# Fourteen weight remainders by an accumulating DMA, and the last router scores one slot later

## The reference

```
x = x + block1(layernorm(x))     # 4 experts, picked by token id; weights ctx (256 x 256) for gate, up and down
x = x + block2(layernorm(x))     # 8 experts of width 176, top 2 of the router's scores, softmax weights
block: y = (silu(h @ W1.T) * (h @ W2.T)) @ W3.T
```

## Time and profile before

| what | us |
|---|---|
| median of 3 runs | 164.11 (164.03 to 164.11) |
| the profiled execution | 164.04 |
| its span, first to last instruction | 162.2 |
| PE busy with matmuls | 154.5 |
| VectorE busy | 111.7 |
| ScalarE busy | 67.8 |
| POOL busy | 57.2 |

### The profile page before, as it was taken

How to read it: one execution, slowest core, us unless ns; L and a number is a source line. 1 busy time by engine, 2 the same in 40 slices (tenths; PEclk the granted TensorE clock), 3 DMA queues, 4 the chain that set the end, 5 groups by cost and what they waited for, 6 DMA issues and landing times.

```text
span 162.2 us, 2463 instructions
## 1 busy us (share of the span) xinstructions
PE 154.5 (95%) x904; PEld 131.0 (81%) x904; DVE 111.7 (69%) x224; ACT 67.8 (42%) x121; POOL 57.2 (35%) x50
## 2 busy tenths in 40 slices
PE   7999899899999999999999799999999999999991
PEld 2477698789897788888889488888888888888890
DVE  0878999785986756799999947917444744444453
ACT  3385775754618622474335812324222222222210
POOL 0679956469767480555467310000000000000000
PEclk9999999999999999999999999999999999999999
DMA  3976353032030003033000000000000300000003
GB/s 107 349 246 191 82 203 107 0 97 76 29 97 0 2 0 101 0 97 97 0 4 0 0 0 2 4 0 0 0 0 4 129 0 0 0 2 4 0 0 129
DMA packets 4620, 8.76 MB, mean 54 GB/s; under 512 B 768, under 2 KB 1408, under 8 KB 4608
## 3 DMA queue, kind: packets, MB, share of 16 engines
q1 hardware_dynamic: 4176, 8.34, 16.3%
q10 hardware_dynamic: 432, 0.27, 0.5%
HBM read 7.55 MB, written 1.05 MB: 53 GB/s over the span
## 4 chain that ended last, share of the span: by engine, by line
PE 65%; DVE 21%; issue 4%; ACT 4%; POOL 3%; DVEq 0%; ACTq 0%; POOLq 0%
PE z L685 36%; PE y L710 22%; DVE act L587 5%; PE z L720 4%; DVE act_lo L552 4%; DVE norm L485 2%; DVE w_lo L558 2%; POOL gated L337 2%; DVE stats L468 2%; DVE hT_lo L492 1%; ACT act_hi L388 1%; ACT silu L416 1%; POOL rstd L299 1%; PE y L627 1%; DVE x_sb L498 1%
## 5 line engine op out<-in xcount | busy, mean ns | idle before, releaser
L685 PE MATMUL z<-hT_hi,w_hi 128*128 128x512 f32 x120 | 47.4, 395 | 1.1 <-ACT hT_hi L362 0.9
L685 PE MATMUL z<-hT_hi,w_lo 128*128 128x512 f32 x120 | 47.1, 393 | 0.0
L710 PE MATMUL y<-w_hi,act_lo 128*128 128x256 f32 x152 | 43.5, 286 | 1.0 <-DVE act_lo L552 0.9
L552 DVE TENSOR_TENSOR act_lo<-act,act_hi 128x512 fp32r<-128x512 f32 x38 | 33.6, 884 | 14.8 <-ACT act_hi L388 14.5
L710 PE MATMUL y<-w_hi,act_hi 128*128 128x256 f32 x152 | 43.0, 283 | 0.0
L710 PE MATMUL y<-w_lo,act_hi 128*128 128x256 f32 x152 | 42.9, 283 | 0.0
L416 ACT ACTIVATE silu<-z 128x512 f32<-128x512 f32 x38 | 22.6, 595 | 41.1 <-PE z L685 41.1
L685 PE MATMUL z<-hT_lo,w_hi 128*128 128x512 f32 x120 | 37.3, 392 | 0.0
L289 POOL TENSOR_TENSOR w_lo<-raw,w_hi 128x768 fp32r<-128x768 f32 (+1 forms) x15 | 27.5, 1845 | 20.3 <-ACT w_hi L353 18.9
L388 ACT CAST act_hi<-act 128x512 fp32r<-128x512 f32 x38 | 23.4, 617 | 19.7 <-DVE act L587 19.4
L710 PEld LDWEIGHTS y<-w_hi,act_lo 128*128 128x128 f32 x152 | 29.0, 191 | 3.2 <-DVE act_lo L552 1.5
(11 more groups left out here) (52 smaller groups left out, 80.8 us busy)
## 6 DMA issues: line engine op xcount, KB each, us to landing
raw<-weights_dram SPq DMA_DIRECT2D x11, 384.0 KB, 3.1
raw<-weights_dram SPq DMA_DIRECT2D x8, 256.0 KB, 4.5
x_sb<-x_dram SPq DMA_DIRECT2D x4, 256.0 KB, 4.4
out_dram<-x_sb SPq DMA_DIRECT2D x2, 256.0 KB, 2.5
out_dram<-x_sb SPq DMA_DIRECT2D x2, 128.0 KB, 2.0
out_dram<-x_sb ACTq DMA_DIRECT2D x2, 128.0 KB, 2.1
consts_sb<-consts_dram SPq DMA_DIRECT2D x1, 68.0 KB, 3.7
ids_sb<-token_ids_dram ACTq DMA_DIRECT2D x1, 4.0 KB, 3.9
```

The source lines that it names most:

```text
L552: nc.vector.tensor_tensor(act_lo[:, i, :], act[:, i, :], act_hi[:, i, :].bitcast(F32), ALU.subtract)\
L685: return nc.tensor.matmul(bank[:], w[b][:, c, cols], tokens[:, h, k, :], **flags)
L710: last = nc.tensor.matmul(o, a[:, q % BUFFERS, rows], w[b][:, c, wd], start=(first and j == 0), stop=(c == CHUNKS[b] - 1 and j == 2), skip ...
```

## The change

After it VectorE subtracts (0,0) alone, POOL (0,1) to (0,4), and the other 14, (0,5) to (0,7) and all 11 of block 2, are made in two moves. ScalarE, right after it has rounded the piece, writes the rounded piece negated into `w_lo` (a Copy with scale -1 into a float32r tile). Then POOL, where it would have subtracted, issues a DMA that adds the piece's weights from DRAM to that tile. `up` waits for the DMA's own semaphore. SP's reload of a raw buffer now waits for the negated pass instead of the remainder. (1,3) is no longer put off by a step on POOL. Apart from this, the last scores (half 1 of block 2) go from slot 0 to slot 1 of step 23, that is behind down(20).

```diff
-    "scores": (None, (7, 0), (7, 0)),
+    "scores": (None, (7, 0), (7, 1)),
...
-VECTOR_LO = ((0, 0), (0, 5), (0, 6), (0, 7))
-
-
-LATE_LO = (1, 3)
+VECTOR_LO = ((0, 0),)
+POOL_LO = ((0, 1), (0, 2), (0, 3), (0, 4))
+
+
+def by_dma(b, c):
+
+
+    return (b, c) not in VECTOR_LO + POOL_LO
+
...
+        w_lo_in = [[sem(f"w_lo_in{b}_{c}") if by_dma(b, c) else None for c in range(CHUNKS[b])] for b in range(2)]
+        w_negated = sem("w_negated")
...
         def wait_lo(engine, b, c):
 
-            vector = [p for p in VECTOR_LO if p <= (b, c)]
             if (b, c) in VECTOR_LO:
-                engine.wait_ge(w_lo_vector, len(vector))
+                engine.wait_ge(w_lo_vector, VECTOR_LO.index((b, c)) + 1)
+            elif (b, c) in POOL_LO:
+                engine.wait_ge(w_lo_pool, POOL_LO.index((b, c)) + 1)
             else:
-                engine.wait_ge(w_lo_pool, piece_no(b, c) - len(vector))
+                engine.wait_ge(w_lo_in[b][c], 16)
+
+        def negated_no(b, c):
+
+            return piece_no(b, c) - len(VECTOR_LO) - len(POOL_LO)
...
+                    last = (0, n) if n < CHUNKS[0] else (1, n - CHUNKS[0])
+                    if by_dma(*last):
+
+                        sp.wait_ge(w_negated, negated_no(*last))
+                    else:
+                        wait_lo(sp, *last)
...
+            def add_weights(b, c):
+
+                pool.wait_ge(w_negated, negated_no(b, c))
+                nc.gpsimd.dma_start(w_lo[b][:, c, :], (weights1, weights2)[b][:, c, :], accum_op=ALU.add)\
+                    .then_inc(w_lo_in[b][c], 16)
...
-                if LATE_LO in SPLIT_AT.get(q - 1, ()):
-                    weight_lo(*LATE_LO)
                 for piece in SPLIT_AT.get(q, ()):
-                    if piece not in VECTOR_LO and piece != LATE_LO:
+                    if by_dma(*piece):
+                        add_weights(*piece)
+                    elif piece in POOL_LO:
                         weight_lo(*piece)
...
                 nc.scalar.copy(w_hi[b][:, c, :], raw_piece(b, c)).then_inc(w_hi_done, 1)
+                if by_dma(b, c):
+                    nc.scalar.activation(w_lo[b][:, c, :], raw_piece(b, c), ACT.Copy, scale=-1.0).then_inc(w_negated, 1)
```

More of the change, by code:

```diff
@@ L252, in load_piece @@
                     n = piece_no(b, c) - RING - 1
-                    wait_lo(sp, *((0, n) if n < CHUNKS[0] else (1, n - CHUNKS[0])))
+                    last = (0, n) if n < CHUNKS[0] else (1, n - CHUNKS[0])
[3 more added lines that the diff above has]
+                        wait_lo(sp, *last)
                 sp.dma_start(raw_piece(b, c), (weights1, weights2)[b][:, c, :]).then_inc(w_in[b][c], 16)
@@ L324, in _ @@
             for c in range(FIRST_PIECES):
-                if (0, c) not in VECTOR_LO:
+                if (0, c) in POOL_LO:
                     weight_lo(0, c)
```

## The result

| | before | changed |
|---|---|---|
| median of 20 runs, us | 164.25 (164.03 to 165.06) | 166.18 (164.65 to 167.09) |
| ratio, 95% interval | | 1.0104 (1.0080 to 1.0129) |
| profiled execution / its span | 164.04 / 162.2 | 165.29 / 163.5 |
| PE, DVE, ACT, POOL busy | 154.5, 111.7, 67.8, 57.2 | 154.6, 103.0, 77.1, 46.2 |

The forecast was 163.4, range 162.3 to 165.2, with 0.23 on slower. The changed kernel's runs fall into two groups: 9 of 164.65 to 165.87 us at a granted clock of 0.996 or more, and 11 of 166.13 to 167.09 at 0.985 to 0.99. The two groups' medians are 165.53 and 166.87. The profile is of the first group. It can explain the 1.25 us by which it is longer than the profiled execution before, out of 1.93 between the medians; most of the rest comes from the second group.

A forecast was written before the change was run, and what follows sets the result against it. TensorE, busy 154.5 of 162.2 us, was taken as the bound. Delay 0.57 and scores -1.27 gave -0.7 us: 163.3 from the profiled 164.04, with the median 0.07 higher 163.4, range 162.3 to 165.2.

The forecast's parts named there:

- The unit costs: TensorE: six products of a block 1 up step 1.39 us, twelve of block 2 2.75, a down step 1.43.
- the list of holes: TensorE waits before down(1) 0.86, up(8) 0.84, down(11) 0.63 and the last scores 1.27: about 3.6 us to win.
- The last scores: Last scores moved behind down(20): either part alone cures the hole before them, together they cure it once, -1.27 us.
- ScalarE: 14 added negated passes, 0.55 us for 128x512 and 0.74 for 128x768, 9.8 us in sum; (1,0)'s on the path to up(8).
- the walk: Steps 1 to 3 followed engine by engine with an issue of 0.9 us: up(8) at 33.05, 1.2 us later.
- The issue, d: Time POOL takes to issue one DMA: taken as 0.9 us, between 0.46 and 1.85.
- rival B: POOL's issue is dear, 1.85 us, in front of gated in steps 1 to 3: up(8) +2.8, total 165.0; chance 0.15.
- So act_lo(1) runs 18.2 to 18.9: VectorE, without w_lo(0,5), does act_lo(1) unhindered; down(1) starts at 19.36 and its 0.86 hole closes.
- I take 4.5 and a bit and cost it at nothing: Landing of (0,5) by DMA, from POOL's taking up the issue at 17.9: costs nothing up to 5.9 us.
- rival C: The accumulating DMA lands late, 9.0 us after 17.9: up(8) 4.3 late, total 166.5; chance 0.09.
- From there the old spacing holds: After gated(5), 0.47 late, spacing unchanged but for the new 0.74 pass: up(8) at 33.05, 1.2 us later.
- The hole closes: +1.2 - 0.63: Before down(11): act_lo(11) ready near 51.8, TensorE asks at 52.3, so the delay from there on is +0.57.

The follow-up runs named there:

- e1: Kernel before with only the last scores moved behind down(20): 162.94 us, ratio 0.9913.
- e10: Changed kernel with (0,5), (0,6), (0,7) back on VectorE and (1,0) on POOL, so DMA for (1,1) to (1,10) only: 162.54 us, ratio 0.9889.
- e11: Kernel of e10 with (0,7) by DMA too, SP's loads of (1,1) and (1,2) held until it has landed: 161.98 us, ratio 0.9840.
- e2: Changed kernel with the last scores back in slot 0, ahead of down(20): 166.75 us, in two groups of runs.
- e9: Kernel of e7 with a POOL product of 128x512 in each probe step, in even steps behind an accumulating issue: act 2.50 us in step 28.
- e13: Kernel of e9 with POOL started from up(q) and two or three small products ahead of the issue: act_lo 2.62 us in one even step.
- e7: Kernel of e1 with eight 256 KB DMAs added on POOL in steps 28 to 35, accumulating and plain in turn: 162.85 us.
- e5: Changed kernel with SP's loads of (1,1) and (1,2) held until (0,6) landed: 8 of 13 runs 163.72 to 164.08 us, five 168.2 to 168.9.
- e12: Changed kernel where POOL issues (0,6), ahead of gated(3), only when act_lo(1) is done: 165.41 us.
- e6: Changed kernel with POOL's 14 DMAs as plain copies, the addition left out: 162.79 us.
- e3: Changed kernel with (0,5), (0,6), (0,7) back on VectorE, only block 2's pieces by DMA: 163.35 us, ratio 0.9929.
- e8: Changed kernel where POOL issues (0,5) only once act_lo(1) is done: 168.92 us.
- e4: Changed kernel with block 2's eleven remainders back on POOL, only (0,5), (0,6), (0,7) by DMA: 166.81 us.

## Why the prediction was wrong, step by step

**The unit costs and the list of holes: right.** e1 won what the last of the four holes holds, and e10 closed the third as well. The first two still stand in e10 (0.58 and 0.59 idle). The whole 3.6 us was reached by no run; e11 came to 2.5.

**The last scores: right.** -1.27 forecast; down(11) to up(24) took 43.08 - 41.85 = 1.23 less. e1 and e2 show that each part alone does it.

**ScalarE: right.** (0,5)'s pass, silu(2) and act_hi(1) came within 0.1 us of the walk; act of the second block fell to 0.68 (mean of 22).

**The issue, d: near, and on the high side.** 0.9 forecast; POOL's next instruction starts 0.83 after the first issue and 0.62 after the others. A dear issue (rival B) wasn't the cause.

**"So act_lo(1) runs 18.2 to 18.9": the first step that failed.** It took 2.67 us, and down(1) came at 20.88 instead of 19.36. I had used the rule that a two-operand VectorE instruction stands while POOL runs a product, and looked only at whether a product *was running* at 18.2. With the issue in front, the product that stood next in POOL's queue already kept it out (e9 and e13; the issue by itself doesn't, e7). The Trainium skill ("SBUF — State Buffer", section "Who interferes with whom") says that a VectorE instruction with two SBUF inputs contends with a GpSimd instruction that reads SBUF, and that the order of issue decides who blocks. The rows agree: in the kernel before, act_lo starts 0.11 us first, keeps its 0.68 and the product stands; in e9's odd steps the product is first, keeps its 1.29, and act_lo stands. That a queued product counts from the issue in front of it on is what e9 and e13 add.

In the profiled execution this hold cost the total nothing that shows: PE stood 1.71 us before up(5) as well, for the DMA, and would only have stood there longer. It costs where it happens twice. In 11 of 20 runs act_lo(1) presumably lost to gated(3) too: this is seen in e2's and e5's profiles, and gone in e12. PE then idles 3.4 us, its granted clock falls to the lower level of 1.2 GHz (e2: 0.64, 0.50, 0.50 and 0.65 in the four us from 24), and the run is 1.3 us longer (group medians 165.53 and 166.87). The prediction had no such case.

**"I take 4.5 and a bit and cost it at nothing": the second, and the one that decides.** (0,5) landed 6.4 us after POOL took it up (17.87 to 24.23), past the limit of 5.9 that the step itself set. (0,6), for which the prediction worked out no limit, took 7.6 (19.96 to 27.60). So PE idled 1.71 and 0.29 us, and up(8) started at 34.27, 2.42 late instead of 1.2. Of the 1.22 between, 0.47 is up(5) past 23.8, 0.44 the wait for (0,6), and 0.31 slower first products. That was rival C, at 0.09, in a milder form than priced. The mistake was to read the earlier trace rows's DMA slices of before as the company of the new transfers, and the median of SP's landings as theirs. Even these were read too low: the 5 in that row means 50 to 60%, and from 20 to 24 us the share was 0.61, where the prediction held against rival C that "no slice of the DMA row is over half full after 16 us". The changed kernel then fills the engines from 20 to 28 us, since each added byte costs 1.8 times a copied one (e6) and SP's loads share them (e5: 4.35 and 4.60 us with these held back): (1,1) and (1,2), released as before, and (1,3), released 2.2 us earlier by the change.

**"From there the old spacing holds", and so 1.2 us later: too high, and the landing hid it.** e6 has the passes and the issues and adds nothing, and its up(8) is 0.42 late. Its act_hi(5) starts at 28.51, against 29.38 before, since VectorE no longer has its three subtractions; that gives back more than the pass of 0.74 costs. The walk left it out. So up(8) was 1.22 later than forecast only because this error and the landing's cancelled in part: against e6, the slower landings cost 2.0 us there.

**"The hole closes: +1.2 - 0.63": the third step that failed.** It grew, from 0.52 us (0.63 with the slow first product) to 0.89: PE was free at 52.58 + 0.79 and started at 54.26. down(11) came 2.62 late (54.26 against 51.64) instead of 0.57. e3, 0.8 late, shows the step's chain working, with a router remainder of 0.17; at 1.2 late, which the step assumed, no run shows it. In the changed kernel the sum of block 1 waits for PE's down(7) and comes 2.2 us later than before, and the remainder meets gated(11) and takes 1.60 us, so that nothing is left that absorbs. In e8, e5, e2 and e12, with up(8) 2.4 to 6 us late, up(8) to down(11) takes 19.97 to 19.99 us, as in the changed kernel (20.00): there the lateness goes through whole.

**The sum.** Forecast -0.70 for the profiled execution, measured +1.25. The landings, net of the walk's error: 34.27 - 33.05 = 1.22; the hole that didn't close: 2.62 - 2.42 + 0.63 = 0.83; scores 0.04; behind up(24) it was 0.14 shorter than before. Together the 1.95 by which it missed. The median lies 0.9 above the profiled execution, mostly by the longer group.

## What to carry to other kernels

A transfer's price is what the engines will be doing in the kernel *after* the change: add up what the same moment releases, the loads that the change itself lets go earlier included, and price an accumulating DMA's time on the engines at nearly two copies. Count a POOL product that stands behind a DMA issue as if it ran from the issue on, for VectorE's instructions with two SBUF operands. Where such an instruction is on the path, make POOL wait for it, but ahead of an issue that nothing urgent needs (e12), not ahead of the urgent one (e8). And before writing off a delay against a later hole, follow that hole's chain back: where it starts from the late engine, only what is taken out of the chain absorbs anything.

## What the runs showed that was not expected

- Plain DMA of 256 KB issued by POOL, alone: 3.0 to 3.3 us; accumulating: 3.9 to 4.3 (e7); accumulating among the loads: 6.3 to 7.6 (changed kernel). The accumulating ones of 384 KB: 6.0 to 6.7 us for the first seven, 4.7 to 5.0 for the last four, when SP has no loads left (changed kernel).
- VectorE's instruction can be passed over repeatedly: 4.94 us of standing in front of a POOL queue of issue, gated, issue, gated (e2), and whether it is differs from run to run. In the two profiles with the long stand act_lo(1) starts 0.14 to 0.15 us after the issue, in the profiles of the changed kernel, e4, e6 and e12 0.28 to 0.29; that this decides it isn't shown. Between two products with no issue it was not passed over: in the kernel before, act_lo(1) stands through gated(2) only, and gated(3), right behind, waits for it.
- One idle of TensorE of 3.4 us is followed by a granted clock of 0.57 over the next 4 us (e2); idles of 1.24 and 1.71 us, 3 us apart, by none (changed kernel, 1.00 from 20 to 32 us).
